# Attention inside a fused cross-attention and feed-forward kernel: the softmax matrix turned by VectorE and DMA in place of TensorE transposes, and the values product moved behind the next scores

## The reference

```python
h_q = (rmsnorm(x) @ w_q.T).reshape(b, lq, H, DH)      # H = 32, DH = 128
h_k = (ctx @ w_k.T).reshape(b, lk, H, DH)
h_v = (ctx @ w_v.T).reshape(b, lk, H, DH)
score = einsum('bqhd,bkhd->bhqk', h_q, h_k) + position_bias[None]
score = where(m, score, -inf); score = softmax(score, axis=-1); score = where(m, score, 0)
attn = einsum('bhqk,bkhd->bqhd', score, h_v).reshape(b, lq, H * DH)
x = x + attn @ w_out.T
```

## Time and profile before

| | |
|---|---|
| median of 3 timed runs | 943.55 us (943.39 to 945.39) |
| span of the profiled execution | 942.7 us |
| TensorE busy | 933.8 us, 99% of the span |
| VectorE, ScalarE, GpSimd busy | 629.9, 409.5, 520.2 us |
| moved by DMA | 171.70 MB, mean 182 GB/s |

### The profile page before, as it was taken

How to read it: one execution, slowest core, us unless ns; L and a number is a source line. 1 busy time by engine, 2 the same in 40 slices (tenths; PEclk the granted TensorE clock), 3 DMA queues, 4 the chain that set the end, 5 groups by cost and what they waited for, 6 DMA issues and landing times.

```text
span 942.7 us, 16961 instructions
## 1 busy us (share of the span) xinstructions
PE 933.8 (99%) x5517; PEld 816.1 (87%) x5517; DVE 629.9 (67%) x1161; ACT 409.5 (43%) x1143; POOL 520.2 (55%) x582
## 2 busy tenths in 40 slices
PE   9999999999999999999999999999999999999997
PEld 7888898888888888888888888988898888878885
DVE  5666664466766576756766676657665767886787
ACT  5664434344343434333434344334434344335664
POOL 3450724457565756584757565856567553133477
PEclk9999999999999999999999999999999999999999
DMA  9315327674667365745676376637673666230101
GB/s 329 110 55 177 121 116 267 215 254 153 227 228 264 119 256 197 280 150 207 221 268 204 137 268 240 212 133 279 217 271 133 224 207 224 69 123 1 35 23 68
DMA packets 61291, 171.70 MB, mean 182 GB/s; under 512 B 6056, under 2 KB 8492, under 8 KB 60989
## 3 DMA queue, kind: packets, MB, share of 16 engines
q1 hardware_dynamic: 61244, 171.11, 51.6%
HBM read 159.56 MB, written 11.53 MB: 181 GB/s over the span
## 4 chain that ended last, share of the span: by engine, by line
PE 94%; DVE 2%; ACT 1%; issue 1%; POOL 1%; DMA 1%; SPq 0%; ACTq 0%; DVEq 0%; POOLq 0%
PE ps_q L355 7%; PE ps_q L357 7%; PE ps_q L356 7%; PE ps_o L355 6%; PE ps_o L357 6%; PE ps_o L356 6%; PE ps_k L355 6%; PE ps_k L357 6%; PE ps_v L355 6%; PE ps_k L356 6%; PE ps_v L357 6%; PE ps_t L2183 6%; PE ps_v L356 6%; PE ps_s L2156 6%; PE ps_t L2173 3%
## 5 line engine op out<-in xcount | busy, mean ns | idle before, releaser
L780 ACT ACTIVATE scores<-scores,neg_max 128x128 f32<-128x128 f32 x256 | 99.8, 391 | 219.9 <-DVE neg_max L1583 219.8
L1470 DVE TENSOR_TENSOR acc<-ps_o,acc 128x512 f32<-128x512 f32 x128 | 87.8, 686 | 60.9 <-PE ps_o L357 60.9
L355 PE MATMUL ps_o<-wo_hi,att_hi 128*128 128x512 f32 x256 | 105.9, 414 | 0.0
L357 PE MATMUL ps_o<-wo_hi,att_lo 128*128 128x512 f32 x256 | 100.3, 392 | 0.0
L356 PE MATMUL ps_o<-wo_lo,att_hi 128*128 128x512 f32 x256 | 100.0, 390 | 0.0
L786 ACT COPY probs_t<-ps_t 128x512 f32<-128x512 f32 x64 | 37.7, 588 | 139.5 <-PE ps_t L2173 139.4
L1104 POOL TENSOR_TENSOR shift<-bias_sb,mask_sb 128x512 f32<-128x512 f32 x64 | 84.8, 1326 | 2.9 <-DVE scores L1579 2.9
L1458 DVE TENSOR_TENSOR att_lo<-ps_t,att_hi 128x512 fp32r<-128x512 f32 x64 | 44.2, 691 | 55.2 <-ACT att_hi L773 55.2
L1145 POOL TENSOR_TENSOR wq_lo<-raw_q,wq_hi 128x256 fp32r<-128x256 f32 x65 | 48.1, 740 | 58.9 <-ACT wq_hi L612 58.9
L355 PE MATMUL ps_v<-wv_hi,ct_hi 128*128 128x256 f32 x264 | 75.1, 284 | 0.4 <-POOL wv_lo L1125 0.3
L357 PE MATMUL ps_v<-wv_hi,ct_lo 128*128 128x256 f32 x264 | 74.7, 283 | 0.0
(11 more groups left out here) (394 smaller groups left out, 2780.9 us busy)
## 6 DMA issues: line engine op xcount, KB each, us to landing
ring_hi<-scratch_x_t SPq DMA_DIRECT2D x39, 512.0 KB, 4.0
ring_lo<-scratch_x_t SPq DMA_DIRECT2D x39, 512.0 KB, 4.9
ring_hi<-scratch_c_t SPq DMA_DIRECT2D x39, 512.0 KB, 4.0
ring_lo<-scratch_c_t SPq DMA_DIRECT2D x39, 512.0 KB, 5.3
raw_o<-in_w_o SPq DMA_DIRECT2D x16, 512.0 KB, 4.9
raw_q<-in_w_q SPq DMA_DIRECT2D x15, 512.0 KB, 6.4
raw_k<-in_w_k SPq DMA_DIRECT2D x15, 512.0 KB, 7.1
xt_hi<-scratch_x_t SPq DMA_DIRECT2D x13, 512.0 KB, 7.3
```

What stands on the lines that cost most here:

```text
L355: pe.matmul(dst, hi_l, hi_r, start=first, stop=False)
L357: return pe.matmul(dst, lo_l, hi_r, start=False, stop=last)
L780: e = act.activation(probs[n][:, m, :], scores[n][:, m, :], ACT.Exp, bias=neg_max[:, n, m:m + 1], accum_out=row_sum[:, n, m:m + 1])
L1470: dve.tensor_tensor(acc[:, b, :], ps_o[:], acc[:, b, :], ALU.add).then_inc(o_added, 1)
```

## The change

1. `step_transpose` and `pt_evac` go, except for step 63.
2. In their place the scores are stored by DVE so that keys k = 4r + j lie in block j at place r (`by_block`); the exponentials and the factor work on that order; a DVE transpose turns the whole 128x512 tile in 32x32 blocks, in place; and ACT's queue issues four transfers a step (`pt_exchange`), each from 32 partitions of `scores[n]` to all 128 of `probs_t`, in rows of 512 bytes.
3. `step_values(s - 1)` stands directly behind `step_scores(s)` on PE, and waits for the four transfers.
4. On DVE `attention_rest(s - 1)` moves from the head of the step to behind `softmax_front(s)`. ACT keeps its order.

```diff
             def exponentials(s, n):
                 act.wait_ge(s_neg, s + 1)
-                wait_from(act, pt_done, s - 1)
                 for m in range(4):
-                    e = act.activation(probs[n][:, m, :], scores[n][:, m, :], ACT.Exp,
+                    tile = scores[n][:, m, :] if isinstance(s, int) and s == STEPS - 1 else by_block(scores[n])[:, :, m, :]
+                    e = act.activation(tile, tile, ACT.Exp,
                                        bias=neg_max[:, n, m:m + 1], accum_out=row_sum[:, n, m:m + 1])
...
+            def pt_exchange(s, n):
+                act.wait_ge(p_done, s + 1)
+                for i in range(4):
+                    act.dma_start(probs_t[:, i, :], scores[n][i * Q:(i + 1) * Q, :, :]).then_inc(pt_in, 16)
...
-                pt_evac(s)
+                pt_exchange(s, n)
...
# DVE, softmax_front and softmax_back (all steps but the last)
                 wait_from(dve, e_done, s - 1)
+                wait_from(dve, pt_in, 64 * (s - 1))
...
+                    dve.tensor_tensor(by_block(scores[n]).rearrange("p j m r -> p m r j"),
+                                      ps_s[:].rearrange("p (m r j) -> p m r j", m=4, j=4),
+                                      shift[n][:].rearrange("p m (r j) -> p m r j", j=4), ALU.add).then_inc(s_shifted, 1)
...
+                    dve.tensor_reduce(row_max[:, n, :], by_block(scores[n]).rearrange("p j m r -> p m j r"), AX_XY,
+                                      ALU.max).then_inc(s_chain, 1)
...
+                    dve.tensor_tensor(by_block(probs[n]), by_block(probs[n]),
+                                      row_fac[:, n, :].unsqueeze(1).unsqueeze(3).broadcast_to([P, 4, 4, Q]),
+                                      ALU.mult).then_inc(s_chain, 1)
+                    dve.wait_ge(s_chain, 4 * s + 4)
+                    dve.transpose(flat(probs[n]), flat(probs[n])).then_inc(p_done, 1)
...
# DVE, step
-                attention_rest(s - 1)
...
                 softmax_front(s, n)
+                attention_rest(s - 1)
...
# PE, step_values
-                pe.wait_ge(pt_out, s + 1)
+                    pe.wait_ge(pt_in, 64 * (s + 1))
+                    wait_from(pe, att_lo_s, s)
...
# PE, step: the same regrouping stands in the steps written out
                 step_scores(s, c)
+                if c == 0:
+                    step_values(s - 1, 7, v_count(i - 1, 14))
+                elif static and s <= 4 * PLAIN:
+                    step_values(s - 1, c - 1, s - 1 - (c - 1) % 2 + 2)
+                elif not own:
+                    step_values(s - 1, c - 1, 16)
+                else:
+                    step_values(s - 1, c - 1, v_count(i, (1, 2, 11, 12, 13, 14, 14)[c - 1]))
...
-                step_transpose(s, c)
                 output(s - 1, (c - 1) % LOOP_STEPS, None, (1,))
-                if static and s < 4 * PLAIN:
-                    step_values(s, c, s - c % 2 + 2)
...
# PE, the end: values(62) behind scores(63), output(62, part 0) behind product_g(0)
             step_scores(s, 7)
-            output(s - 1, 6, None, (0,))
+            step_values(s - 1, 6, v_count(TURNS - 1, 14))
             spread_kb()
...
             product_g(0)
+            output(s - 1, 6, None, (0,))
             small_pair(0)
```

More of the change, by code:

```diff
@@ L25 @@
 AX_X = mybir.AxisListType.X
+AX_XY = mybir.AxisListType.XY
 P = 128
@@ L46 @@
 MASKED = 3e38
+Q = 32
 SCORE_SCALE = float(D) ** -0.5
@@ L899, in _ @@
             wk1_high_part(2)
-            pt_evac(STEPS - 4)
+            pt_exchange(STEPS - 4, 0)
             wk1_high_part(3)
@@ L912, in _ @@
             wq1_high_part(1)
-            pt_evac(STEPS - 3)
+            pt_exchange(STEPS - 3, 1)
             wq1_high_part(2)
@@ L926, in _ @@
             exponentials(STEPS - 2, 0)
-            pt_evac(STEPS - 2)
+            pt_exchange(STEPS - 2, 0)
             attention_high(STEPS - 2)
@@ L1832, in unpack_code @@
                                   ALU.bitwise_and).then_inc(unp, 1)
-            attention_rest(STEPS - 3)
             wq1_rest(3)
             softmax_front(STEPS - 2, 0)
+            attention_rest(STEPS - 3)
             add_output(STEPS - 3, 5, (0,))
@@ L1856, in _ @@
             softmax_front(STEPS - 1, 1)
+            attention_rest(STEPS - 2)
             add_output(STEPS - 2, 6, (0,))
@@ L2176, in step_values @@
             def step_values(s, c, made):
-                pe.wait_ge(pt_out, s + 1)
+                whole = isinstance(s, int) and s == STEPS - 1
+                if whole:
+                    pe.wait_ge(pt_out, PT_ALL + 1)
+                else:
+                    pe.wait_ge(pt_in, 64 * (s + 1))
+                    wait_from(pe, att_lo_s, s)
                 pe.wait_ge(v_out, made)
@@ L2182, in step_values @@
                         m = 2 * j + h
+                        moving = probs_t[:, m, :] if whole else flat(probs_t).rearrange("p (i m c) -> p i m c", i=4, m=4)[:, :, m, :]
                         last = pe.matmul(ps_t[:, m * P:(m + 1) * P], vv[n][:, 2 * (c % 2) + j, h * P:(h + 1) * P],
-                                         probs_t[:, m, :], start=True, stop=True)
+                                         moving, start=True, stop=True)
                 last.then_inc(pv_done, 1)
@@ L2453, in step @@
                     v_p2(i + 1, 1)
-                step_transpose(s, c)
                 output(s - 1, (c - 1) % LOOP_STEPS, None, (1,))
-                if static and s < 4 * PLAIN:
-                    step_values(s, c, s - c % 2 + 2)
-                elif not own:
-                    step_values(s, c, 16)
-                else:
-                    step_values(s, c, v_count(i, (1, 2, 11, 12, 13, 14, 14, 14)[c]))
                 if c % 4 == 0 and not (last and c == 4):
```

47 lines of the change are left out of this document (25 added, 22 removed).

## The result

The changed kernel takes 1124.01 us (median of 4 runs, 1122.4 to 1130.34) against 944.47 for the kernel before in the same series: a ratio of 1.192, 95% interval 1.188 to 1.195. The forecast of 995 us had the direction and most places right, and the size wrong by far: +180 us in place of +52.

What follows compares the result with a forecast made beforehand. TensorE, busy for 99% of the span, was taken as the bound: -27.7 + 13.5 + 22.4 + 10.8 + 7.3 + 4.4 + 16.1 + 5 = +51.8 on 942.7, so 995 us with 0.85 around it; range 955 to 1030.

Steps and rivals of the forecast that it cites:

- The transfers: Values product waiting for the exchange behind positions 7 and 3: 2.9 and 4.5 us free, 5.0 needed; +16.1 us.
- L: Time from `p_done` to the exchange's last landing: 3.15 to 9.65 us, taken as 5.0.
- the 1 us of step 1: In step 1 the values wait for the first exchange: about +1 us.
- The late rival: Last landing like SP's 6.5 us load gives 1030 us, with 8.5 1056; chance 0.14 for transfers later than the main case.
- Any time for which PE is made to wait costs in full: TensorE, busy for 99% of the span, bounds the kernel, so each wait put on it adds its length.
- ACT issues four transfers ... so nothing: On ACT, four issues of 0.33 to 0.49 us stand ahead of casts not yet due; cost nothing.
- The chain: Links from values product to output: 0.5 us at positions 0, 1, 3, 5; 3.2 at 2; 1.8 and 1.2 at 6; 0.7 at 7.
- the ends: Step 63's ACT instructions queued behind earlier rounding and output part 0 moved, +4 us; step 1's wait, about +1; 5 in the sum.
- The transposes: Four TensorE transposes and the longer product behind them go, 0.44 us a step in 63 steps: -27.7 us.
- VectorE slow: Rival: strided write, and perhaps the DVE transpose, take 1.22 us instead of 0.69; 1016 to 1022 us, chance 0.13.
- Part 0 isn't held: Rival: `att_lo` comes in time for output part 0; 941 us, or 925 with the exchange hidden too; chance 0.10.
- transfers hidden: Rival: the exchange lands within 2.9 us of `p_done`, its 16.1 us go; 979 us, within the main case's range (chance 0.60).

Runs made afterwards that it cites:

- e1_order: The changed kernel without the exchange: only its new order stays, with TensorE transposes, `pt_evac` and the old VectorE patterns; 1013.8 us, ratio 1.074.
- e3_one: The changed kernel with one transfer of the four a step, so the values product works on wrong probabilities; 1059.3 us, ratio 1.124.
- e10_copy: The changed kernel with one ScalarE copy for the four transfers, blocks not exchanged, so the product works on wrong probabilities; 1015.8 us, ratio 1.076.
- e17_late3_copy: The changed kernel reordered to give the exchange a whole step of slack, values products later, one ScalarE copy for the four transfers (wrong probabilities); 932.9 us, ratio 0.988.
- e8_plain: The changed kernel with the VectorE patterns of before ahead of the DVE transpose, so what is exchanged isn't the transposed softmax; 1120.7 us, ratio 1.186.

## Why the prediction was wrong

The span grew by 177.9 us where 51.8 were forecast. The 126 between are 54.5 of waits for transfers (70.6 for 16.1), 12.5 of waits for `wv_lo`, 7 in all the other waits, and 52 of time in which TensorE was busy, for which the forecast had no term but the transposes.

- **The step that failed first is "The transfers"**: L = 5.0 from `p_done` at +16.1 us. Measured at position 7 is 530.0 - 520.5 = 9.5, just under the upper bound of 9.65 that the text had; the four issues took 2.65 us in place of about 1.6, and the landing was that of a transfer beside SP's eight, which the text named and then set aside "since these don't queue behind SP's". At L = 9.65 the forecast's own rule gives 6 x 6.75 = 40.5 us behind position 7; the six waits seen add up to 39.8 (6.4 to 6.9 each). Behind position 3 it gives 36 where 14.7 are seen, and 14 us of waits for transfers in turn 0 and the last turn had only the 1 us of step 1. The exchange's DMAs cost 108 us (1124.0 - 1015.8). The late rival, at 8.5 for the landing, gave 1056: right in kind, and still 68 short.
- **"Any time for which PE is made to wait costs in full" is too low**: a wait costs more than itself, and no case had that. TensorE's clock falls in the long waits: 2.6 us of slow products follow the wait at position 0 each time, and up to 1.8 follow that at position 2 in some turns, in *e1_order* too, without any transfer. And about 0.3 us goes at each restart.
- **"ACT issues four transfers ... so nothing" is wrong**: the casts `wv_hi` come behind 2.5 to 2.65 us of issues, GpSimd's `wv_lo` behind them, 12.5 us of PE's waits in all. With 0.6 us of issues, in *e3_one*, and with the copy of *e10_copy*, they aren't among the waits of 0.9 us or more.
- **The chain** held: positions 1, 3 and 5 at 0.60, 1.10 and 0.87 us for 0.5, position 2 3.10 for 3.2, position 6 1.72 for 1.8 and its part 1 0.98 for 1.2, position 7 0.99 for 0.7. Position 0, forecast at 0.5, isn't held behind its long wait. In *e1_order* the waits for `att_lo` come to 44.6 for 46.7. That the order alone cost 70 us, where 46.7 and 5 for the ends make 52, is the slower products again: TensorE is busy for 19 us more there (952.8 for 933.8).
- **The transposes** are worth what was said, but only if nothing takes it: in *e10_copy* the longer VectorE chain did, in *e17_late3_copy* 11 us of it remained.
- **VectorE slow** as a rival: the strided write is slow (1.06), and the time barely depends on it (3 us in *e8_plain*, with overlapping intervals). The prediction priced it at +21 to +27.
- **"Part 0 isn't held"** fell, as did "transfers hidden".

What stays open: how a short transfer takes its turn beside SP's stream. One took 6.4 us and four 7.2 with the same stream beside them, and the one landed 1.7 us ahead of a transfer that SP had issued 0.3 us earlier. The Trainium skill (DMA: Bandwidth & Descriptors, Queues, rings and completion order) has the engines take turns between queues by packet; the early landing agrees with that, the small gain from a quarter of the packets doesn't. Open too is the split between issues and landing over the whole kernel: no run issued the transfers without waiting for them. And it is open why the clock falls behind a wait of 2.78 us in some turns and not in others that look the same.

## What to carry to other kernels

A transpose by DMA takes nothing from TensorE and puts a latency into the loop; ask how many microseconds lie between producer and consumer at the shortest step of the loop, and price the landing by the worst row of traffic that is issued there, not by the middle. When a product is moved across a step, list for each engine what is queued behind the instruction that waits for it: here one copy behind `attention_high` was worth 46 us. And where an engine at 99% is made to wait, the wait is not the whole price: here 154 us more of waits came with 52 us more of busy time.

## What the hardware showed

- A transfer of 64 KB between partitions, 128 rows of 512 bytes: 0.55 us or more to issue on ScalarE's queue (SP's of 512 KB 0.33 to 0.49), 2.1 us to land with nothing beside it, 3.5 in the median, 7.1 to 7.4 in the median of four behind eight transfers of SP, and 7.9 at most.
- The granted clock fell to 1.2 GHz in the waits of 6.6 us at position 0, before TensorE worked again, and behind some of the waits of 3.1 us at position 2, not behind all; in *e1_order* behind waits of 2.78 us in three turns of five.
- The VectorE transpose of 128x512 in 32x32 blocks takes 0.71 us; a sum of this size that writes with a step of 128 elements 1.06.
